# A graph attention layer on one core: VectorE's order within a step of the edge loop, and its table look-up in two parts

## The reference

```
q = (x @ Wq.T + bq).reshape(N, 32, 8) * 32 ** -0.5      # k and v likewise, without the factor
s = einsum('edh,edh->eh', q[src], k[dst])
m = segment_max(s, src);  e = exp(s - m[src]);  z = segment_sum(e, src)
out = segment_sum((e / z[src])[:, None, :] * v[dst], src)
y = layernorm(x + out.reshape(N, -1) @ Wo.T + bo)
```

## Time and profile before

| | |
|---|---|
| median of 3 runs | 4026.59 us (4025.29 to 4100.18) |
| the profiled execution | 4017.71 us |
| its span, first to last instruction | 4015.6 us |
| VectorE busy | 3211.0 us, 80% |
| GpSimd busy | 2447.6 us, 61% |
| TensorE busy, mean granted clock | 2227.2 us, 55%; 0.743 |
| ScalarE busy | 1504.6 us, 37% |

### The profile page before, as it was taken

One profiled execution on the slowest core, in us unless ns is written; L12 is line 12 of the kernel. 1 busy time (PEld: TensorE's weight loads), 2 busy tenths in 40 slices (PEclk: granted clock), 3 DMA queues, 4 the chain that ended last, 5 costly groups with the idle time before them and its releaser, 6 DMA issues. The chain is left out here.

```text
span 4015.6 us, 59591 instructions
## 1 busy us (share of the span) xinstructions
PE 2227.2 (55%) x7109; PEld 1514.8 (38%) x7109; DVE 3211.0 (80%) x8164; ACT 1504.6 (37%) x6480; POOL 2447.6 (61%) x2365
## 2 busy tenths in 40 slices
PE   3999888653002555555555545555555555544776
PEld 3788775432001333333333333333333333323443
DVE  8554467799223999999999999999999999977776
ACT  0110002221001555555555555555555555534332
POOL 3221120003767777777777777777777777765677
PEclk9966568776555788778777787777877778766777
DMA  1211013226513788878887887888777788799222
GB/s 33 64 58 32 16 43 101 89 67 125 171 36 96 231 233 232 232 232 232 231 232 232 232 232 231 232 232 231 232 232 231 232 232 232 229 177 169 80 92 85
DMA packets 329217, 665.86 MB, mean 166 GB/s; under 512 B 63462, under 2 KB 191750, under 8 KB 329016
## 3 DMA queue, kind: packets, MB, share of 16 engines
q0 software_dynamic: 160768, 518.27, 46.4%
q1 hardware_dynamic: 168392, 146.96, 12.7%
HBM read 599.35 MB, written 65.86 MB: 166 GB/s over the span
## 5 line engine op out<-in xcount | busy, mean ns | idle before, releaser
L931 POOL DMA_INDIRECT kv<-kv_rows,idx x1794 | 1863.0, 1038 | 583.7 <-issue 538.5
L1032 PE MATMUL sum_ps<-pv,ident 128*128 128x264 f32 x2392 | 902.0, 512 | 1299.3 <-DVE pv L825 1299.3
L1032 PEld LDWEIGHTS sum_ps<-pv,ident 128*128 128x128 f32 x2392 | 511.3, 237 | 1712.1 <-DVE pv L825 1393.1
L987 ACT ACTIVATE pv<-kv,s 128x33 f32<-128x33 f32 x4784 | 1084.4, 309 | 53.9 <-ACT s L977 27.3
L790 DVE TENSOR_TENSOR prod<-kv,q 128x768 f32<-128x768 f32 x598 | 569.2, 952 | 59.7 <-DMA kv<-kv_rows,idx 59.6
L797 DVE TENSOR_REDUCE s<-prod 128x24 f32<-128x768 f32 x598 | 565.5, 946 | 0.0
L977 ACT ACTIVATE s<-s 128x32 f32<-128x32 f32 x598 | 137.0, 229 | 1126.1 <-DVE s L818 1126.1
L1034 PE MATMUL sum_ps<-pv,ident 128*128 128x264 f32 x1196 | 497.3, 508 | 0.0
L507 PE MATMUL hist_ps<-hot_lo,hot_hi 125*98 125x128 bf16 x1600 | 372.1, 409 | 121.7 <-DVE hot_hi L174 121.7
L825 DVE TENSOR_TENSOR pv<-kv,s 128x528 f32<-128x528 f32 x598 | 417.4, 698 | 0.3 <-ACT s L977 0.3
L507 PEld LDWEIGHTS hist_ps<-hot_lo,hot_hi 125*98 125x98 bf16 x1600 | 370.3, 259 | 123.2 <-issue 68.7
(11 more groups left out here) (164 smaller groups left out, 2450.5 us busy)
## 6 DMA issues: line engine op xcount, KB each, us to landing
q<-q_perm SPq DMA_DIRECT2D x598, 128.0 KB, 3.7
kv<-kv_rows,idx POOLq DMA_INDIRECT x1794, 4.0
kv_rows<-kv_st SPq DMA_DIRECT2D x98, 260.0 KB, 3.0
xt_sb<-in_xT SPq DMA_DIRECT2D x98, 128.0 KB, 3.2
node_rows<-q_st SPq DMA_DIRECT2D x98, 128.0 KB, 3.4
q_perm<-kv_st SPq DMA_DIRECT2D x98, 128.0 KB, 1.9
kv_st<-node_rows,node_id POOLq DMA_INDIRECT x98, 3.1
cols<-edge_keys,run_at POOLq DMA_INDIRECT x98, 2.5
```

The source lines that it names most:

```text
L931: pool.indirect_dma_start(out=kv[:, j, g, :], out_offset=None, in_=kv_rows, in_offset=bass.IndirectOffsetOnAxis(ap=idx[:, j, g:g + 1], axi ...
L987: last = act.activation(pv[:, b, V * VW + at_h:V * VW + at_h + HD + 1], kv[:, j, V, D + at_h:D + at_h + HD + 1], ACT.Copy, scale=s[:, b, V ...
L1032: pe.matmul(sum_ps[b][:, 0:VW], ident[:, :], pv[:, b, g * VW:(g + 1) * VW], start=g == 0, stop=False)
```

## The change

Only VectorE's program in the edge loop is changed; the instructions that compute, their sizes and their buffers are the same. In a step the old order is: score_sum, weigh, look_up, copy of the old maximum, mask, maxima, add_sum, score, scale_acc, differences. The new one is: score_sum, look_up (load only), add_sum, copy of the old maximum, weigh, mask, scale_acc, maxima, score, decode, differences. The copy has a helper of its own, `old_maximum`, and the look-up is split: `look_up` loads the entry into a register, and `decode` takes tile and column from it some instructions later.

```diff
-                def mask_scores(k, b, col, tile):
+                def old_maximum(k, b, tile):
 
                     dve.tensor_copy(s[:, b, G * HEADS:], runmax[:, bass.ds(tile * HEADS, HEADS)]).then_inc(old_copied, 1)
+
+                def mask_scores(k, b, col):
+
                     dve.wait_ge(scored, k + 1)
...
-                def look_up(k, c):
-                    v = dve.value_load(step_tab[0:1, bass.ds(k, 1)], min_val=0, max_val=TAB * C * P - 1)
+                entry_r = dve.alloc_register("entry")
+
+                def look_up(k):
+                    dve.reg_mov(entry_r, dve.value_load(step_tab[0:1, bass.ds(k, 1)], min_val=0, max_val=TAB * C * P - 1))
+
+                def decode(c):
+                    v = bounded(dve, entry_r, TAB * C * P - 1)
                     dve.reg_mov(tile_r[c], v & (P - 1))
                     dve.reg_mov(col_r[c], v >> PBITS)
 
                 def step(k, j, turn, peel=False, last=False):
 
                     b, b1 = j % 2, (j + 1) % 2
-                    score_sum(k + 1, b1, peeled=peel and j == 0)
-                    weigh(k, j % U, b, peeled=peel and j < 2)
-
                     tile, tile1, col1 = (bounded(dve, tile_r[j % 3], TILES), bounded(dve, tile_r[(j + 1) % 3], TILES),
                                          bounded(dve, col_r[(j + 1) % 3], TAB * C - G))
                     before = None if peel and j == 0 else bounded(dve, tile_r[(j + 2) % 3], TILES)
-                    look_up(k + 2, (j + 2) % 3)
-                    mask_scores(k + 1, b1, col1, tile1)
-                    maxima(k + 1, b1, tile1)
+                    score_sum(k + 1, b1, peeled=peel and j == 0)
+                    look_up(k + 2)
                     if before is not None:
                         add_sum(k - 1, b1, before)
+                    old_maximum(k + 1, b1, tile1)
+                    weigh(k, j % U, b, peeled=peel and j < 2)
+                    mask_scores(k + 1, b1, col1)
+                    scale_acc(k, b, tile, first=peel and j == 0)
+                    maxima(k + 1, b1, tile1)
                     if not last:
                         score(k + 2, (j + 2) % U, turn + (j + 2) // U)
-                    scale_acc(k, b, tile, first=peel and j == 0)
+                    decode((j + 2) % 3)
                     differences(k + 1, b1, tile1)
```

More of the change, by code:

```diff
@@ L865, in step @@
                     before = None if peel and j == 0 else bounded(dve, tile_r[(j + 2) % 3], TILES)
-                    look_up(k + 2, (j + 2) % 3)
-                    mask_scores(k + 1, b1, col1, tile1)
-                    maxima(k + 1, b1, tile1)
+                    score_sum(k + 1, b1, peeled=peel and j == 0)
+                    look_up(k + 2)
                     if before is not None:
                         add_sum(k - 1, b1, before)
+                    old_maximum(k + 1, b1, tile1)
[3 more added lines that the diff above has]
+                    maxima(k + 1, b1, tile1)
                     if not last:
                         score(k + 2, (j + 2) % U, turn + (j + 2) // U)
-                    scale_acc(k, b, tile, first=peel and j == 0)
+                    decode((j + 2) % 3)
                     differences(k + 1, b1, tile1)
-                look_up(0, 0)
-                look_up(1, 1)
+                look_up(0)
+                decode(0)
+                look_up(1)
+                decode(1)
                 score(0, 0, 0)
@@ L880, in _ @@
                 tile, col = bounded(dve, tile_r[0], TILES), bounded(dve, col_r[0], TAB * C - G)
-                mask_scores(0, 0, col, tile)
+                old_maximum(0, 0, tile)
+                mask_scores(0, 0, col)
                 maxima(0, 0, tile)
@@ L897, in _ @@
                 add_sum(k, k % 2, tile)
-                for r in tile_r + col_r:
+                for r in tile_r + col_r + [entry_r]:
                     dve.free_register(r)
```

## The result

The changed kernel takes 4183.16 us (median of 4, 4180.31 to 4189.92). The ratio to the kernel before is **1.038, 95% interval 1.034 to 1.042: slower**. The kernel before, run beside it, had a median of 4035.74 us in 4 runs. A kernel's runs fall into an undisturbed group and a slower one (the kernel before: 4014 to 4069 us, and 4083 to 4210), and all ratios here compare undisturbed runs. The changed kernel's profiled execution takes 4182.9 us with a span of 4181.0, against 4017.7 and 4015.6.

The account below looks back on a forecast made before the run. VectorE was taken to pace the loop at 4.01 us a step, 0.10 above GpSimd's floor. 552 x (4.45 - 4.01) = +243 us on the profiled 4017.7 gave 4261, plus 9 for the runs' median: 4270; range 4000 to 4385.

Parts of the forecast that it names:

- VectorE's own step: VectorE's edge-loop step without waits: predicted to fall from 3.97 to 3.65 us, bounds 3.55 and 3.80.
- GpSimd's floor: Edge loop: three undelayed gathers at 1.30 us each, so GpSimd needs at least 3.91 us a step.
- the ring: Level stretch: product holds third gather, whose late rows delay the next product; 4.34 to 4.66 us a step.
- The look-up: VectorE's step: moved under the 0.87 us reduction, costed at nothing; if uncovered, the add starts up to about 0.2 us late.
- the rival in which VectorE doesn't get quicker: Look-up or semaphores keep VectorE's step at 3.95 to 4.1 us: 3995 to 4076, about 4030 us; chance 0.16.
- The size of the held state: Level stretch with gathers held by products: 4.45 us a step instead of 4.01, +243 us over 552 steps.
- the state renews itself: Level stretch: each held third gather lands late, the next product waits, and the next third gather is held again.
- the landing: Arrival of gathered rows: from a held gather's end to the product's start, 2.51 or 2.83 us.
- The mixture that I forecast: Half-clock stretches rebuild slack, full-clock ones spend it: 4.15 to 4.3 us a step, 4104 to 4187 us; chance 0.08.
- my likeliest case: Gathers held by products throughout the level stretch: forecast 4270 us, own range 4200 to 4390; chance 0.64.
- The wait of the add: Add ahead of pv waits for TensorE's sums: 4.35 us round at half clock, 2.95 at full, hidden in the held state.
- The signs that I named: Level stretch: product waits near 0.8 us, a third of gathers 1.4 to 1.8 us, mean 1.2, transfers 209 GB/s.

Follow-up runs that it names:

- run 1: Kernel before with only the look-up split, its load behind the reduction and its decoding behind the product: 4186.22 us, ratio 1.040.
- runs 3 and 8: An unused VectorE reduction added ahead of the product: 0.68 us more on run 2, 4121.29 us; 0.28 us on run 1, 4007.01 us.
- run 4: Changed kernel with the product's second operand a constant in PSUM, q left out of the scores: 4081.88 us, ratio 1.014.
- runs 5 and 7: Large second operands put in PSUM, computation complete: on the order of run 2, 3955.27 us; on the changed order, 3942.39 us.
- run 2: Changed kernel with the add put back behind weighing and mask, and the accumulator's scaling behind maxima: 4266.00 us, ratio 1.061.
- runs 2 to 6: Those from run 2 on, the last being the kernel before with its large second operands in PSUM: 3991.25 us, ratio 0.991.

## Why the prediction was right, and where it was off

- **Direction and mechanism: right.** Slower, by gathers held under VectorE's instructions with two SBUF inputs, as soon as VectorE's own step falls below GpSimd's floor. The trace shows the ring, run 1 sets it off with a small saving, runs 3 and 8 undo it with added work, run 4 takes 101 us of it away by moving one operand, and runs 5 and 7 take away all of it.
- **The Trainium skill's rule on the shared port** (SBUF — State Buffer, "Who interferes with whom") is borne out by run 4 for what a gather waits for: the same instruction with one input in PSUM holds none. That an instruction with at most one SBUF input, outside the modes that take both ports, doesn't contend is stated there as well. The same section also has `tensor_tensor` not stalling a DMA that GpSimd issues, for a reason that it calls inferred; the 264 gathers held by the product show otherwise for indirect ones, and the measurement decides.
- **GpSimd's floor, right.** 3.91 was read from free gathers, and runs 5 and 7 stand at 3.91. What the product's tail costs a step in the kernel before I read as 0.06 us from one gather; over the window it is 3 x (1.032 - 0.998) = 0.10.
- **VectorE's own step: 3.65 said, 3.58 measured.** Three terms were off. The reduction behind the product I made 0.12 dearer, 0.22 after differences; it starts 0.12 after them: -0.10. The copy gives way to pv after 0.07, where I left it its 0.14: -0.07. The look-up I costed at nothing under the reduction; the add starts 1.00 us after the reduction's start instead of 0.87, so 0.13 of it sticks out. The rest is 0.03 in small pieces. So the rival in which VectorE doesn't get quicker falls, with its 0.16.
- **The size of the held state: the term that failed.** I took 4.45 us a step and 4.33 was measured, which is 68 of the 78 us by which 4261 lay above the profiled 4182.9. The ring itself is as long as said where it closes (4.59 and 4.38 above). What failed is "the state renews itself": the product holds a gather in 264 of 462 steps, some 57%. The term behind it is the landing. From a third gather's end to the product that waits for its rows I took 2.51 or 2.83 us for a held gather and 2.73 for a free one, from the first steps of the loop; in the window the medians are 2.87 (222 steps) and 3.18 (127). The next third gather is due 2.91 us after that end (0.305 and two free gathers of 1.303), and later only by what the first two gathers are held, so a late landing puts it ahead of the product, where it is free. In the 123 steps in which the product started less than 2.86 us after the end, the next third gather was held every time; in the other 339, 141 times.
- **The mixture that I forecast is another one.** I had given it 0.08, with 4104 to 4187, and my likeliest case 4200 to 4390, and the result lies in the mixture's range. But its condition was that half-clock stretches rebuild the slack and full-clock ones spend it, and the trace doesn't show that: the product holds a gather in 92 of 163 steps that lie wholly at half clock, and in 63 of 120 wholly at full clock. That its range fits is luck.
- **The wait of the add** was expected as hidden, 4.35 in a step of 4.45. It shows as 0.15 us a step (70.1 us in 462 steps), and taking it away (run 2, which moves the scaling too) made the kernel slower.
- **Outside the loop** I let nothing change. The end, whose code is the same, became 14 us shorter, and the padding 6 longer.

The signs that I named came, most of them smaller than said: waits of the product with the DMA as releaser (324 of 462, 0.51 us a step against 0.8 said), longer gathers (1139 ns, about 1.2 us said; 1.4 us and more in a fifth of them, a third said), transfers down (215 GB/s, 209 said).

## What to carry to other kernels

When VectorE and GpSimd run side by side, an instruction of VectorE with two SBUF inputs can hold GpSimd's next indirect DMA to its end. Look at the spread of GpSimd's records before the order of VectorE is made tighter: here a mean above the 998 ns of a free record was held time, and with GpSimd near to being the bound it added to the step in full. The cure in this kernel was to put one of the two operands into PSUM, where an engine with room can write it. And when one engine paces another by a small margin, find out what happens once it stops doing so: here 0.1 us of margin kept 0.3 us of stalls away.

## What the runs showed of the hardware that was not expected

- A reduction of 0.28 us that computes nothing made a 4186 us kernel 179 us faster, and one of 0.68 us another one 145 us faster.
- A gather is held only if it starts at some distance behind the start of the product. In run 1, 42 gathers started 0 to 44 ns after a product's start and none was held; 211 started 45 ns or more after it, up to shortly before its end, and all were held.
- VectorE's products, reading one operand from PSUM, last as long as from SBUF: 948 to 952 ns against 951.
- The end of the kernel has mostly two lengths, whatever the loop: about 300 us (before, runs 2 to 6) or 286 to 288 (after, runs 1 and 7), and 292.5 in run 8. There the gathers of x take 1150 ns in the kernel before and 1032 in the changed one. Their 98 records make up 11.5 of the 14.4 us:

```profile
L1178 POOL DMA_INDIRECT x<-in_x_rows,node_id x98 | 112.7, 1150 | 56.9 <-issue 30.7 <-SPq L1078 22.8 <-DVE y L1105 2.1
```

```profile
L1190 POOL DMA_INDIRECT x<-in_x_rows,node_id x98 | 101.2, 1032 | 58.9 <-issue 28.5 <-SPq L1090 23.5 <-DVE res L1122 3.8
```

The second is the changed kernel's. What decides between the two was not tried.
